# DLRM tower on one core: the second layer in two halves with a bank each, and another order in the last chunk's gram steps

## The reference

```python
e = jnp.stack([tbl_0[ids[:, 0]], ..., tbl_25[ids[:, 25]]], axis=1)
sd = jnp.einsum('bfd,bd->bf', e, dense)
ss = jnp.einsum('bfd,bgd->bfg', e, e)
pairs = ss[:, iu, ju]
z = jnp.concatenate([dense, sd, pairs], axis=1)
h = jnp.concatenate([z, dense], axis=1)
h = jnp.maximum(h @ W_top1 + b_top1, 0.0)
h = jnp.maximum(h @ W_top2 + b_top2, 0.0)
y = h @ W_top3
```

## Time and profile before

| | us |
|---|---|
| median of three runs | 368.14 |
| lowest and highest | 367.41, 368.69 |
| the profiled execution | 368.76 |
| its span | 367.0 |
| TensorE busy in it | 330.2 (90%) |
| GpSimd busy | 253.1 (69%) |
| VectorE busy | 237.5 (65%) |
| ScalarE busy | 186.7 (51%) |

### The profile page before, as it was taken

One profiled execution on the slowest core, in us unless ns is written; L12 is line 12 of the kernel. 1 busy time (PEld: TensorE's weight loads), 2 busy tenths in 40 slices (PEclk: granted clock), 3 DMA queues, 4 the chain that ended last, 5 costly groups with the idle time before them and its releaser, 6 DMA issues.

```text
span 367.0 us, 14291 instructions
## 1 busy us (share of the span) xinstructions
PE 330.2 (90%) x6236; PEld 305.5 (83%) x6236; DVE 237.5 (65%) x703; ACT 186.7 (51%) x270; POOL 253.1 (69%) x269
## 2 busy tenths in 40 slices
PE   0777499968999999989999999999999999989886
PEld 0766399967999899979999899989998899978774
DVE  1999999753984498644984497747876397313031
ACT  2345756535637365436637365446644464655432
POOL 5777777777777777777777777777777777774000
PEclk9999789989999999999999999999999999999999
DMA  7999834365445443554436443554346533531000
GB/s 172 249 246 239 261 99 112 99 150 134 103 108 127 127 115 83 131 126 126 109 83 146 131 106 86 132 129 127 103 100 140 141 92 78 123 101 45 5 2 0
DMA packets 41163, 43.92 MB, mean 120 GB/s; under 512 B 25694, under 2 KB 30154, under 8 KB 41100
## 3 DMA queue, kind: packets, MB, share of 16 engines
q1 hardware_dynamic: 32700, 25.81, 28.5%
q0 software_dynamic: 8384, 17.19, 18.5%
q10 hardware_dynamic: 16, 0.01, 0.0%
HBM read 38.13 MB, written 4.85 MB: 117 GB/s over the span
## 4 chain that ended last, share of the span: by engine, by line
PE 55%; POOL 20%; issue 9%; DMA 5%; ACT 5%; DVE 4%; SPq 1%; POOLq 0%; ACTq 0%; DVEq 0%
PE et_ps L611 23%; POOL rows L395 20%; PE g_ps L633 10%; PE m_ps L585 8%; PE m_ps L674 6%; PE et_ps L603 5%; DMA gram<-tbl_in 3%; DVE one_hot L513 3%; ACT et L435 2%; DMA et<-tbl_in 2%; ACT et L427 2%; PE m_ps L683 2%; DVE table_lo L502 1%; DMA rows<-tbl_in,idx 1%; PE et_ps L643 1%
## 5 line engine op out<-in xcount | busy, mean ns | idle before, releaser
L395 POOL DMA_INDIRECT rows<-tbl_in,idx x262 | 252.3, 963 | 82.0 <-issue 78.1
L513 DVE TENSOR_SCALAR one_hot<-idb,first_row 125x256 fp32r<-125x256 int32 x616 | 193.5, 384 | 58.8 <-PE et_ps L611 26.7
L611 PE MATMUL et_ps<-one_hot,table_hi 125*128 125x256 f32 x616 | 159.7, 297 | 15.0 <-DVE one_hot L513 14.9
L611 PE MATMUL et_ps<-one_hot,table_lo 125*128 125x256 f32 x616 | 152.9, 285 | 0.0
L611 PEld LDWEIGHTS et_ps<-one_hot,table_hi 125*128 125x128 f32 x616 | 119.5, 194 | 18.1 <-issue 10.8
L611 PEld LDWEIGHTS et_ps<-one_hot,table_lo 125*128 125x128 f32 x616 | 120.0, 195 | 0.1
L435 ACT COPY et<-et_ps 128x512 f32<-128x512 f32 (+1 forms) x66 | 81.4, 1247 | 24.9 <-PE et_ps L603 22.7
L427 ACT COPY et<-et_ps 128x256 f32<-128x256 f32 (+1 forms) x78 | 46.6, 719 | 52.2 <-PE et_ps L611 52.2
L633 PE MATMUL g_ps<-et 128*27 128x26 f32 x4096 | 60.2, 193 | 11.2 <-issue 6.4
L633 PEld LDWEIGHTS g_ps<-et 128*27 128x27 f32 x4096 | 49.3, 105 | 24.6 <-issue 11.3
L448 ACT COPY gram<-g_ps 128x416 f32<-128x416 f32 x32 | 29.7, 929 | 51.1 <-PE g_ps L633 51.0
(11 more groups left out here) (58 smaller groups left out, 205.7 us busy)
## 6 DMA issues: line engine op xcount, KB each, us to landing
idb<-ids_one_hot SPq DMA_DIRECT2D x38, 256.0 KB
gram_rows<-gram SPq DMA_DIRECT2D x28, 169.0 KB
rows<-tbl_in,idx POOLq DMA_INDIRECT x262
et<-tbl_in SPq DMA_DIRECT2D x6, 448.0 KB
xt<-dense_t SPq DMA_DIRECT2D x8, 128.0 KB, 2.9
raw<-tbl_in SPq DMA_DIRECT2D x2, 448.0 KB
gram<-tbl_in SPq DMA_DIRECT2D x2, 448.0 KB
zt_raw<-gram_rows SPq DMA_DIRECT2D x14, 48.0 KB
```

The source lines that it names most:

```text
L395: nc.gpsimd.indirect_dma_start(out=rows[:, i % ROW_RING, n, :], out_offset=None, in_=tables[COLUMNS[field + n]], in_offset=bass.IndirectOf ...
L513: nc.vector.tensor_scalar(one_hot[0:KP, at % OH_RING, :], idb[0:KP, pair % ID_RING, n % 2, :], first_row[0:KP, 0:1], float(k), ALU.subtrac ...
L611: last = nc.tensor.matmul(ps[:, n % 2 * CH:(n % 2 + 1) * CH], part[0:KP, n, k, :], one_hot[0:KP, at % OH_RING, :], start=k == 0 and part i ...
```

## The change

M becomes two steps, M0 and M1, of 12 matmuls each: M0 writes the first half to `m_ps[0]`, M1 the second to `m_ps[1]`. Each raises `h2_sums` by itself, and ScalarE evacuates each half behind its own step. Y waits for both halves and writes to `m_ps[0]`. In `PHASE` and `LAST` M1 follows M0 directly. Around the change from the last phase to the tail the order of chunk 6's second and third layers, chunk 7's gram steps and chunk 7's X changes:

- before: M6, G4, Y, G5, G6, X, G7, A0
- after: M6 (first half), G4, M6 (second half), G5, G6, Y, G7, X, A0

For chunk 7 itself M0 and M1 stand together at the end, then Y.

```diff
@@ PHASE, LAST, TAIL
-    "M0 G2 T4 Y0 G3 O1 T5 O2 O3 T6 O4 T7").split()
+    "M0 M1 G2 T4 Y0 G3 O1 T5 O2 O3 T6 O4 T7").split()
-    "M0 G2 T5 Y0 G3 z0 z1 x0 k0 z2 k1 k2 T6 T7 m0").split()
+    "M0 M1 G2 T5 Y0 G3 z0 z1 x0 k0 z2 k1 k2 T6 T7 m0").split()
-    "G4 Y0 G5 G6 x0 G7 A0 A1 A2 A3 V0 A4 A5 z0 V1 A6 z1 k0 V2 z2 k1 k2 m0 y0").split()
+    "G4 M1 G5 G6 Y0 G7 x0 A0 A1 A2 A3 V0 A4 A5 z0 V1 A6 z1 k0 V2 z2 k1 k2 m0 m1 y0").split()
@@ ScalarE
-                    wait(act, h2_sums, c)
+                    wait(act, h2_sums, 2 * c)
...
                 if kind == "M":
-                    act.wait_ge(h2_sums, c + 1)
+                    act.wait_ge(h2_sums, 2 * c + n + 1)
                     wait(act, y_out, c * 16)
-                    for m in range(2):
-                        last = nc.scalar.activation(h2[:, m, :], m_ps[0][:, m * CH:(m + 1) * CH], ACT.Relu,
-                                                    bias=b2s[:, m:m + 1])
-                    last.then_inc(h2_done, 1)
+                    nc.scalar.activation(h2[:, n, :], m_ps[n][:, 0:CH], ACT.Relu, bias=b2s[:, n:n + 1])\
+                        .then_inc(h2_done, 1)
                 if kind == "Y":
                     act.wait_ge(y_sums, c + 1)
-                    nc.scalar.copy(y, m_ps[1][0:1, 0:CH]).then_inc(y_copied, 1)
+                    nc.scalar.copy(y, m_ps[0][0:1, 0:CH]).then_inc(y_copied, 1)
@@ TensorE
                 if kind == "M":
-                    for m in range(2):
-                        for k in range(4):
-                            if m == 0 and k == 0:
-
-                                pe.wait_ge(h1_split, 2 * c + 1)
-                            if m == 0 and k == 2:
-                                pe.wait_ge(h1_split, 2 * c + 2)
-                            for a, b in ((0, 0), (1, 0), (0, 1)):
-                                last = nc.tensor.matmul(m_ps[0][:, m * CH:(m + 1) * CH],
-                                                        w2_parts[a][:, k, m * 128:(m + 1) * 128],
-                                                        h1_parts[b][:, k, :],
-                                                        start=k == 0 and (a, b) == (0, 0),
-                                                        stop=k == 3 and (a, b) == (0, 1))
+
+                    for k in range(4):
+                        if n == 0 and k % 2 == 0:
+                            pe.wait_ge(h1_split, 2 * c + k // 2 + 1)
+                        for a, b in ((0, 0), (1, 0), (0, 1)):
+                            last = nc.tensor.matmul(m_ps[n][:, 0:CH], w2_parts[a][:, k, n * 128:(n + 1) * 128],
+                                                    h1_parts[b][:, k, :], start=k == 0 and (a, b) == (0, 0),
+                                                    stop=k == 3 and (a, b) == (0, 1))
                     last.then_inc(h2_sums, 1)
                 if kind == "Y":
-                    pe.wait_ge(h2_done, c + 1)
+                    pe.wait_ge(h2_done, 2 * c + 2)
                     for k in range(H2 // 128):
-                        last = nc.tensor.matmul(m_ps[1][0:1, 0:CH], w3s[:, k:k + 1], h2[:, k, :],
+                        last = nc.tensor.matmul(m_ps[0][0:1, 0:CH], w3s[:, k:k + 1], h2[:, k, :],
                                                 start=k == 0, stop=k == H2 // 128 - 1)
```

## The result

The changed kernel took 365.82 us (median of 17 runs), the kernel before 367.41 (17 runs). The ratio is 0.9948, 95% interval 0.9926 to 0.9970: 1.9 us faster (0.0052 x 367.41; the two medians lie 1.6 apart), between 1.1 and 2.7. One disturbed run of 443 us is left out of the ratio. A second comparison of the same two kernels gave 0.9921 (0.9892 to 0.9950).

The account below looks back on a forecast made before the run. TensorE was taken to bound the kernel, busy 330.2 of 367.0 us. Gains of 1.03 us in the tail and 0.37 in chunk 7 sum to 1.4, giving 366.7 us against the median of 368.14; range 365.5 to 368.1.

Parts of the forecast that it names:

- Part 1: Second layer in two halves with a bank each: gain 0.37 us in chunk 7, 0 in chunks 0 to 5.
- A new wait at G4: Tail: G4 waits for ScalarE's copy of the last transposed tile and starts at 341.15, 0.45 us late.
- The place of the stop: Tail: PE reaches the code-block boundary at the 123rd of the 128 weight loads of G5 and G6.
- The gap again: PE's stop in G6: the block comes 0.8 us earlier, at 345.5, and PE still waits 0.8 us.
- The reading under that step: PE's instruction blocks, some 254.5 instructions each: passing a boundary orders the next block, but one step ahead.
- the second rival: PE's stop in the tail: the block still comes at 346.32; gain 0.6 us, 367.5 us; chance 0.23.
- the wait on y: Tail, x behind G7: x waits for y's copy, which ends level with G7; 0.1 us added.
- The evacuation under x: Tail: G7's evacuation is done at 348.15 under x, so A0 no longer waits; 0.96 us at stake.
- the first: Rival for the tail: the gap does not come back, G5, G6, Y, G7 run through; 2.2 us, 365.9; chance 0.22.
- The third, starved gram steps: Rival for G6 and G7: holes between weight loads lose 4.4 us against the gapless 2.2 gained; 370.3 us; chance 0.05.

Follow-up runs that it names:

- second run of the kernel: The changed kernel timed and profiled once more, nothing altered; ratio 0.9921 to the kernel before.
- Y by halves: Changed kernel, with Y's first two matmul records waiting only for the first half of h2, the other two for the second; ratio 0.9942 to the kernel before.
- increments: Extra semaphore increments that nobody waits for, put at the head of PE's stream to shift code-block boundaries; ratios to the kernel before 0.9955 (60), 0.9986 (85), 1.049 (190).
- x kept in front: Changed kernel, but with x ahead of G7 as before and Y behind G5; ratio 0.9984 to the kernel before.
- the kernels with 85 and with 190 of them: Changed kernel plus 85 increments and Y's records waiting by halves, 0.9986 to the kernel before; changed kernel plus 190 increments, 1.049.
- 60: Changed kernel plus 60 semaphore increments at the head of PE's stream; ratio 0.9955 to the kernel before.

## Why the prediction was right and wrong

**The direction and most of the walk were right; when the block comes was not, and so neither was the size.** 366.7 us is 0.7 below the 367.41 that 17 runs of the kernel before give; measured are 1.9. Two things make the difference. The forecast of 1.4 us was set against 368.14, a median of three that lay 0.7 above that of 17. And the 1.4 itself should have been 2.2 by the stretches.

- **Part 1.** Right to the last digit: 0.37 us at the end (4.07 to 3.70), nothing in chunks 0 to 5, nothing for the change of bank.
- **A new wait at G4.** Right: G4 starts 2.07 us behind M6, as worked out (341.15 less 339.08); the second half let G5 start at 4.37 (4.38).
- **The place of the stop.** Right: the 123rd of G5's and G6's loads.
- **The step that failed is "The gap again".** It said that the block comes 0.8 us earlier than before, 6.4 us behind M6. It came 1.39 earlier, at 5.86 (5.91 in the second run of the kernel, 6.04 with Y by halves). I took 0.12 to 0.2 off for the 24 instructions by which the boundary moves behind G4's start; they cost nothing. The block's packet starts 1.41 to 1.64 us behind G4's start in both orders (nine profiles without increments). And I held the rest of the way fixed, while it varies: the packet took 1.33 us before and 0.98 after. That is 0.56 of the 0.78 us by which A0 came earlier than forecast.
- **The reading under that step failed with it**, that passing a boundary orders the next block. The 24 instructions were priced at a gram step's 4.9 ns, but they are the second half's matmuls, which start 0.12 us apart. Counted back 254.5 to 256 instructions from the stop, the boundary lies at the matmul of 344.98 or the one behind it, 3.7 to 3.8 us behind M6; before, it was at the 120th instruction of G4, at 3.6. So PE passes it no earlier than before, and by the reading the block would have come no earlier either, as the second rival has it. But the packet starts at 344.78, ahead of that matmul, where before it started 1.0 us behind the boundary. The forecast of an earlier block thus came out of a wrong price, and that it pointed the right way is luck. What came earlier is G4, by 0.99 us, and the packet with it; what orders a block stays open.
- The rest, 0.2 us, is behind the stop: x started level with G7's end, so the 0.1 us for the wait on y was not there, and the steps ran a little closer.
- **The evacuation under x.** Right: A0 has no wait; with x kept in front the wait of 0.96 is back.

**The rivals.** The gap did come back, so the first fails as a mechanism, though its 2.2 us is by chance the size of the gain. The Trainium skill ("Runtime: NRT & Kernel Launch", Instruction fetch mechanics), which calls the crossing mostly hidden, does not hold for a run of gram steps: ten profiles show a stop of 0.30 to 2.47 us at a block's boundary. The second rival had the block come no earlier; in the kernels that keep M6 whole ahead of G4 it indeed ends at 7.15 to 7.25, but G4's place moves it. The third, starved gram steps, did not occur in the tail of the changed kernel: G7 behind Y ran in 1.03 us. Holes that name no releaser and fit no block do stand elsewhere, though. Before, PE's loads stop for 0.48 us in a gram step ahead of chunk 5's second layer, 9.0 us behind the end of the last code packet; no run here looks into these:

```profile
324.40 0.29 PEld L633 LDWEIGHTS g_ps<-et 128*27 128x27 f32 x19 [0.48 <-issue]
```


What stays open is the total's spread. Executions of one kernel differ by some 4 us, and the profiles place most of it ahead of M6, in stretches that the change leaves alone; why they differ was not studied.

## What to carry to other kernels

Where small matmuls follow each other at 10 ns, count instructions, not only time: find the block boundaries from a stop with no releaser that ends a little over 1 us behind a code packet, and from the number of instructions in a packet, and put slow matmuls (a second layer's half, the third layer) between the dense steps ahead of the boundary. Before a reorder that packs dense steps, work out at which load they reach the boundary and how long before that they start; here G4's start 0.99 us earlier brought the block 1.39 us earlier, though the boundary itself was passed no sooner. An evacuation that the next step needs is best covered with work that needs neither, here x's products, and a long accumulation whose result is read by another engine is cut in two banks only where nothing else covers that read.

## What the hardware showed that was not expected

- PE's stop at a code block's boundary ended 1.26 to 1.48 us behind the end of the block's 16 KB packet in all ten profiles with a stop in this place, and the packet itself took 0.96 to 1.33 us.
- That packet started 0.9 to 1.1 us behind the matmul at the preceding boundary where that stood in G4 (four profiles), but from 0.3 us ahead of it to level with it where it stood in M6's second half (five). In both (kernels without increments) it started 1.41 to 1.64 us behind G4.
- One idle stretch of 2.47 us on PE was followed by about 3.4 us at half the granted clock (0.53 on the mean over 3.6 us); stops of 1.24 and 1.61 us were followed by none (granted clock 1.00 on both sides).
- A semaphore increment on PE's queue took some 0.15 us: between the kernels with 85 and with 190 of them PE's first load moved from 14.52 to 30.58 us (16.06 over 105). 60 cost nothing, since PE waited until 10.7 us anyway.
